# A vision transformer block on one core: V computed once by token, sent through DRAM into a layout by image, and masked by GpSimd

## The reference

```python
h = patchify(x) @ W_proj.T + b_proj + pos_emb          # 16 x 36 x 256, cls_tok ahead: S = 37
qkv = layernorm(h) @ W_qkv + b_qkv
q, k, v = split into 16 heads of 16
att = softmax(causal(q k^T / 4)); out = att @ v         # within one image
h = h + out @ W_out + b_out
z = layernorm(h)                                        # each token goes to one of 8 experts
h = h + score * (gelu(z @ w1[e] + b1[e]) @ w2[e] + b2[e])
```

## Time and profile before

| | us |
|---|---|
| runs shown | 195.72, 196.68, 396.79 |
| their median | 196.68 |
| profiled execution, first to last instruction (span) | 193.6 |
| TensorE busy | 149.7 (77%) |
| VectorE busy | 81.2 (42%) |
| ScalarE busy | 50.5 (26%) |
| GpSimd busy | 30.9 (16%) |
| mean DMA rate over the span | 139 GB/s |

### The profile page before, as it was taken

How to read it: one execution, slowest core, us unless ns; L and a number is a source line. 1 busy time by engine, 2 the same in 40 slices (tenths; PEclk the granted TensorE clock), 3 DMA queues, 4 the chain that set the end, 5 groups by cost and what they waited for, 6 DMA issues and landing times.

```text
span 193.6 us, 2570 instructions
## 1 busy us (share of the span) xinstructions
PE 149.7 (77%) x937; PEld 121.8 (63%) x937; DVE 81.2 (42%) x243; ACT 50.5 (26%) x137; POOL 30.9 (16%) x41
## 2 busy tenths in 40 slices
PE   0006999898499999999984540188999999999980
PEld 0005688676357676686673430178999999999960
DVE  0011002876966678767885348714212022022030
ACT  0002001409513442424432010007421421431400
POOL 1010001496000001001011100430030430420222
PEclk9999999999999999999999655559999999999999
DMA  6999999300000000100681110240059999940000
GB/s 190 372 361 372 377 377 381 107 3 0 0 0 0 2 3 2 54 3 0 186 301 58 56 54 0 71 145 4 0 181 344 352 318 335 349 156 0 18 19 24
DMA packets 15696, 26.99 MB, mean 139 GB/s; under 512 B 2253, under 2 KB 11012, under 8 KB 15552
## 3 DMA queue, kind: packets, MB, share of 16 engines
q1 hardware_dynamic: 12624, 21.89, 32.5%
q0 software_dynamic: 1024, 2.71, 4.2%
q10 hardware_dynamic: 2032, 2.19, 3.4%
HBM read 24.86 MB, written 2.36 MB: 141 GB/s over the span
## 4 chain that ended last, share of the span: by engine, by line
PE 73%; DVE 10%; DMA 8%; issue 2%; ACTq 2%; ACT 2%; POOL 1%; POOLq 0%; DVEq 0%
PE ps L652 16%; PE ps L664 14%; PE ps L515 8%; PE ps L462 8%; DMA bqk<-b_qk 6%; PE ps L532 5%; PE ps L558 4%; PE ps L544 3%; PE ps L606 3%; PE ps L495 3%; PE ps L460 2%; DVE wide L740 2%; DMA early<-hz_scratch,growu 2%; PE ps L535 2%; PE ps L640 1%
## 5 line engine op out<-in xcount | busy, mean ns | idle before, releaser
L652 PEld LDWEIGHTS ps<-early,w1s 128*128 128x128 f32 x256 | 31.7, 203 | 2.2 <-issue 1.9
L652 PE MATMUL ps<-early,w1s 128*128 128x128 f32 x256 | 32.0, 287 | 1.3 <-DVE early L879 1.3
L664 PE MATMUL ps<-w2s,early 128*128 128x256 f32 x128 | 28.8, 379 | 0.0
L431 ACT ACTIVATE early<-ps,b1s 128x128 f32<-128x128 f32 x64 | 18.2, 371 | 31.8 <-PE ps L652 31.8
L664 PEld LDWEIGHTS ps<-w2s,early 128*128 128x128 f32 x128 | 23.8, 190 | 2.9
L952 POOL DMA_INDIRECT out<-early,srowu x8 | 8.1, 1008 | 49.0 <-DVE early L892 49.0
L462 PE MATMUL ps<-early 128*128 128x256 f32 x60 | 14.9, 414 | 0.0
L887 DVE TENSOR_TENSOR ysum<-ps,b2s 128x256 f32<-128x256 f32 x8 | 3.4, 425 | 26.7 <-PE ps L664 26.7
L462 PEld LDWEIGHTS ps<-early 128*128 128x128 f32 x60 | 12.5, 211 | 2.6 <-issue 0.7
L395 ACT ACTIVATE probs<-shifted 101x296 f32<-101x296 f32 x16 | 7.2, 451 | 24.8 <-DVE shifted L762 24.8
L879 DVE COPY early<-ps 128x256 f32<-128x256 f32 x8 | 3.4, 425 | 22.7 <-PE ps L640 22.7
(11 more groups left out here) (125 smaller groups left out, 196.3 us busy)
## 6 DMA issues: line engine op xcount, KB each, us to landing
w1s<-w SPq DMA_DIRECT2D x8, 1024.0 KB, 5.3
w2s<-w SPq DMA_DIRECT2D x8, 1024.0 KB, 9.4
early<-embed_in SPq DMA_DIRECT2D x6, 448.0 KB, 8.9
hz_scratch<-hz SPq DMA_DIRECT2D x5, 256.0 KB, 2.3
b2s<-b ACTq DMA_DIRECT2D x1, 1024.0 KB, 19.9
wqkv<-w_qkv SPq DMA_DIRECT2D x1, 768.0 KB, 13.0
cf<-const_f ACTq DMA_DIRECT2D x1, 642.0 KB, 11.2
wout<-w_out SPq DMA_DIRECT2D x1, 256.0 KB, 13.4
```

Source lines behind the costliest of these rows:

```text
L431: nc.scalar.activation(gt[:, t % 2, f, :], ps[:, 2 * (t % 2) + f // 4, (f % 4) * P:(f % 4 + 1) * P], ACT.Gelu, bias=b1t[:, f:f + 1]).then_ ...
L652: m = nc.tensor.matmul(ps[:, 2 * (t % 2) + f // 4, (f % 4) * P:(f % 4 + 1) * P], w1s[:, r, k, f * P:(f + 1) * P], xt[:, t % 2, k, :], star ...
L664: m = nc.tensor.matmul(ps[:, 4 + t % 2, 0:D], gt[:, t % 2, f, :], w2s[:, r, f, :], start=(f == 0), stop=(f == FT - 1))
```

## The change

V is computed once for each token. `value_rows(j)` on TensorE multiplies a tile of `xnt` by the V columns, ahead of and among the Q and K matmuls. ScalarE copies the result to `vrow`, the first half of `hz`. SP stores it to a DRAM scratch `v_scratch` in two parts (tiles 0 to 2, tiles 3 and 4), waits for each store, and loads it back by image, `[37 rows, 8 images, 256]`, three times a half, to partitions 0, 37 and 74 of `v3`, in the slot where `thrice` was. GpSimd multiplies by `vmask` and writes `vbd`, for all eight pairs, ahead of its adds to `h`. `thrice`, `values` on TensorE and `values` on VectorE go. The load of expert 2 moves behind the V loads, that of expert 3 waits for GpSimd's `v_ready`. scores(0) waits for both parts of Q. The third group of an attend takes its own 34 columns, not 51 for each image.

```diff
+        v_d = nc.dram_tensor("v_scratch", [TP, D], F32, kind="Internal").ap()
-        thrice = [w[:, RING - 1, :, :].rearrange("p a b -> p (a b)")[:, 0:B * GS] for w in (w1s, w2s)]
+        vrow = hz[:, :, 0:D]
+        v3 = [w[0:GS, RING - 1, :, :].rearrange("p a b -> p (a b)").rearrange("p (b d) -> p b d", d=D)
+              for w in (w1s, w2s)]
+        HALF_T = -(-(T // 2) // P)
+        VALUES = ((0, 2, 6), (2, 3, 3), (3, 5, 3))
...
@@ SP
-            for t in range(RING - 1):
-                load_expert(t)
+            load_expert(0)
+            load_expert(1)
+            for g, (j0, j1) in enumerate(((0, HALF_T), (HALF_T, NT))):
+                sp.wait_ge(q["vrow_ready"], j1)
+                sp.dma_start(v_d[j0 * P:j1 * P, :].rearrange("(j p) d -> p j d", p=P), vrow[:, j0:j1, :])\
+                  .then_inc(q["vrow_stored"], 16)
+                sp.wait_ge(q["vrow_stored"], 16 * (g + 1))
+                b0, b1_ = g * B // 2, (g + 1) * B // 2
+                for r in range(GH):
+                    sp.dma_start(v3[g][r * S:(r + 1) * S, :, :],
+                                 v_d[b0 * S:b1_ * S, :].rearrange("(b s) d -> s b d", s=S)).then_inc(loaded_v[g], 16)
+            load_expert(2)
...
-                    sp.wait_ge(q["v_ps"], PAIRS)
+                    sp.wait_ge(q["v_ready"], PAIRS)
...
@@ TensorE
+            def value_rows(j):
+                pe.wait_ge(q["xnt_ready"], j + 1)
+                if j == HALF_T:
+                    pe.wait_ge(q["vrow_ready"], HALF_T)
+                v0, _, bank = next(v for v in VALUES if v[0] <= j < v[1])
+                for k in range(KD):
+                    m = nc.tensor.matmul(ps[:, bank, (j - v0) * D:(j - v0 + 1) * D], xnt[:, k, j * P:(j + 1) * P], wqkv[:, k, 2 * D:3 * D],
+                                         start=(k == 0), stop=(k == KD - 1))
+                m.then_inc(q["vrow_ps"], 1)
...
+                    if a == 0 and n == 1:
+                        pe.wait_ge(q["vrow_ready"], 2)
+                    if a == 1 and n == 2:
+                        pe.wait_ge(q["vrow_ready"], NT)
...
-                    pe.wait_ge(q["q_ready"], u + 1)
+                    pe.wait_ge(q["q_ready"], KD)
...
+                    w = min(GH, HH - g * GH) * VW
...
@@ GpSimd
+            pool.wait_ge(q["v_zeroed"], 2)
+            for pair in range(PAIRS):
+                pool.wait_ge(loaded_v[pair // (PAIRS // 2)], 16 * GH)
+                pool.tensor_tensor(
+                    vbd[:, 2 * pair * VI:2 * (pair + 1) * VI].rearrange("p (h w) -> p h w", w=VW)[:, :, 0:DH],
+                    v3[pair // (PAIRS // 2)][:, 2 * (pair % (PAIRS // 2)):2 * (pair % (PAIRS // 2)) + 2, :].rearrange("p a (h w) -> p (a h) w", w=DH),
+                    C("vmask")[0:GS, :].unsqueeze(2).to_broadcast([GS, 2 * HEADS, DH]), ALU.mult).then_inc(q["v_ready"], 1)
 
             pool.wait_ge(q["loaded_bout"], 16)
             for j in range(NT):
```

More of the change, by code:

```diff
@@ L274, in vit_tower @@
             loaded_bv loaded_bout loaded_b1 loaded_b2 loaded_wg loaded_wred
-            embedded h_saved veps_ready rstd_ready xn_ready xnt_ps xnt_ready thrice_ready
+            embedded h_saved veps_ready rstd_ready xn_ready xnt_ps xnt_ready vrow_ps vrow_ready vrow_stored
             wg_sq wg_norm wgn_ready wgnt_ps wgnt_ready g_ps g_ready bqs_ready
-            qk_ps k_ready q_ready kbd_dve kbd_act v_zeroed v_ps v_ready pads_ready
+            qk_ps k_ready q_ready kbd_dve kbd_act v_zeroed v_ready pads_ready
             scores_ps shifted_ready probs_ready probst_ps probst_ready o_ps o_ready ot_ps ot_ready
@@ L285, in vit_tower @@
         loaded_emb = [sem(f"loaded_emb{k}") for k in range(KE)]
+        loaded_v = [sem(f"loaded_v{g}") for g in range(2)]
         loaded_w = [sem(f"loaded_w{r}") for r in range(RING)]
@@ L362, in _ @@
                 nc.scalar.activation(h[:, j, :], ps[:, j, 0:D], ACT.Copy).then_inc(q["h_saved"], 1)
[L363 to L372, removed]
+            for j0, j1 in ((0, HALF_T), (HALF_T, NT)):
+                for j in range(j0, j1):
+                    act.wait_ge(q["xnt_ps"], j + 1)
+                    nc.scalar.activation(xnt[:, :, j * P:(j + 1) * P],
+                                         ps[:, 5 + 2 * (j % 2), 0:KD * P].rearrange("p (k n) -> p k n", k=KD),
+                                         ACT.Copy).then_inc(q["xnt_ready"], 1)
+                for v0, v1, bank in VALUES:
+                    if j0 < v1 <= j1:
+                        act.wait_ge(q["vrow_ps"], v1)
+                        nc.scalar.activation(vrow[:, v0:v1, :],
+                                             ps[:, bank, 0:(v1 - v0) * D].rearrange("p (j d) -> p j d", d=D),
+                                             ACT.Copy).then_inc(q["vrow_ready"], v1 - v0)
             act.wait_ge(q["bqs_ready"], 1)
@@ L482, in turn_normalised @@
                 m.then_inc(q["xnt_ps"], 1)
+            def value_rows(j):
[7 more added lines that the diff above has]
+                m.then_inc(q["vrow_ps"], 1)
             HALF = T // 2
-            for j in range(-(-HALF // P)):
+            for j in range(HALF_T):
                 turn_normalised(j)
@@ L490, in _ @@
             pe.wait_ge(q["g_ready"], 1)
-            pe.wait_ge(q["xnt_ready"], -(-HALF // P))
+            for j in range(HALF_T):
+                value_rows(j)
             for a in range(2):
                 for n, (col, bank) in enumerate(((D, 0), (D + P, 6), (0, 2), (P, 4))):
+                    if a == 0 and n == 1:
+                        pe.wait_ge(q["vrow_ready"], 2)
+                    if a == 1 and n == 2:
+                        pe.wait_ge(q["vrow_ready"], NT)
                     for k in range(KD):
@@ L499, in _ @@
                 if a == 0:
-                    for j in range(-(-HALF // P), NT):
+                    for j in range(HALF_T, NT):
                         turn_normalised(j)
[L502 to L517, removed]
+                    for j in range(HALF_T, NT):
+                        value_rows(j)
             def scores(u):
@@ L555, in attend @@
                     col = 2 * pair * VI + (c * HH + g * GH) * VW
-                    rhs = early[0:GS, col:col + 2 * VI].rearrange("p (a n) -> p a n", a=2)[:, :, 0:GH * VW]
+                    w = min(GH, HH - g * GH) * VW
+                    rhs = early[0:GS, col:col + 2 * VI].rearrange("p (a n) -> p a n", a=2)[:, :, 0:w]
                     dst = ps[0:ROWS, BO + u % 2, 0:2 * CH * GH * VW].rearrange("p (a n) -> p a n", a=2)
-                    m = nc.tensor.matmul(dst[:, :, g * GH * VW:(g + 1) * GH * VW],
+                    m = nc.tensor.matmul(dst[:, :, g * GH * VW:g * GH * VW + w],
                                          probst[:, u % 2, g * ROWS:(g + 1) * ROWS], rhs, start=True, stop=True)
@@ L568, in _ @@
             pe.wait_ge(q["pads_ready"], 1)
-            values(0)
             for i in range(STEPS):
@@ L572, in _ @@
                     scores(i)
-                    if i % 2 == 0 and i // 2 + 1 < PAIRS:
-                        values(i // 2 + 1)
                 if 0 <= i - 1 < UNITS:
@@ L583, in _ @@
                     pe.wait_ge(q["zt_ready"], j + 1)
-                    if j == EARLY:
-                        pe.wait_ge(q["v_ready"], PAIRS)
                     for k in range(KD):
@@ L741, in _ @@
                                     C("kmask")[:, hd:hd + 1], None, ALU.mult).then_inc(q["kbd_dve"], 1)
[L743 to L753, removed]
             for i in range(STEPS):
```

## The result

The changed kernel takes 259.51 us (259.06 to 261.79, 4 runs) against 196.22 us before: ratio 1.324, 95% interval 1.317 to 1.331. The profiled execution took 259.93 us with a span of 258.1. All ratios here are of the undisturbed executions of either kernel; the one of before that took 396.79 us counts in its median of 196.22 and in no ratio.

A forecast was written before the change was run, and what follows sets the result against it. TensorE was taken to bound the attention loop, VectorE just behind. With the slow V loads, transposed(8) at 140.5 plus 110.5 gives 251.0, plus 2.3 for clock 253.3, plus 3.1 outside the span 256.4 us; range 240 to 270.

The forecast's parts named there:

- One engine for 37 rows: V loads from DRAM: all six share one DMA engine, 46.5 ns a row, 41.3 us a half plus 1.4 fixed.
- two engines for 38 rows: Reading of the early sel transfer: its 38 rows went out on two DMA engines, not on 16.
- The store of half 1 behind half 0: SP's queue: the store of V's half 1 lands only about 1.7 us after half 0's loads, at 88.7.
- Masks: GpSimd's mask of each pair: two 128x256 adds of 0.70 us, 1.4 us for 512 columns.
- The second stall is GpSimd's queue ahead of attend(8): Masks queued ahead of the bout adds hold VectorE's hz of step 7 to 137.9, transposed(8) to 140.5.
- The clock at the restart: After 30 us of standing, TensorE resumes the loop at half clock, booked at 2.3 us.
- the time outside the span: Median less span, 3.1 us in the kernel before, added again to the forecast span of 253.3 us.
- The bounds written for the range: Whole kernel: row pace, clock, store round trip, mask length and lone-engine pace, together 244 to 270 us.
- The first rival: V loads spread over most DMA engines and the change does what it says: 188.1 us, chance 0.07.
- the engines' own gain of 8.6 us: Engines alone: 10.3 us from the loop and 2.0 at its start, less 3.7 for added TensorE matmuls.
- The second rival, the lock: Loads spread, but GpSimd's masks and VectorE's kbd copies shut each other out, some 8 us: 196.1 us, chance 0.04.
- steps near 2.0 us there: Sign of being right: attention loop steps take near 2.0 us between the stalls.

The follow-up runs named there:

- E1: The changed kernel with each load of 37 rows cut into one of 32 rows and one of 5: 200.51 us, ratio 1.019.
- e2: The changed kernel with each load of 37 rows cut into one of 34 rows and one of 3: 220.91 us, ratio 1.124.
- e3: The changed kernel with GpSimd's five adds of bout to h put ahead of its eight masks: 256.39 us, ratio 1.302.
- e9: The changed kernel with GpSimd's adds ahead of all masks and the second normalisation's first power ahead of pair 4's mask: 247.80 us, ratio 1.267.
- e8: The changed kernel with 68 extra matmuls, results unused, ahead of the transposes of unit 8: 255.60 us, ratio 1.300.
- e11: The changed kernel with loads of 32 and 5 rows, masks after the kbd copies, four extra matmuls ahead of each of scores(0) and scores(1): 187.33 us, ratio 0.957.
- e6: The changed kernel with loads of 32 and 5 rows, and GpSimd's masks waiting for VectorE's thirteen kbd copies: 198.58 us, ratio 1.010.
- e5: The changed kernel with loads of 32 and 5 rows, five extra matmuls ahead of scores(0), six ahead of scores(1): 188.87, 200.29, 201.57 and 202.53 us.

## Why the prediction was right, point by point

- **One engine for 37 rows**: right, and the heart of it. Half 0 took 42.6 us where 41.3 + 1.4 = 42.7 was forecast, that is 46.4 ns a row. E1 and e2 show that the outer size decides. This is what the Trainium skill ("DMA: Bandwidth & Descriptors", "Why a DMA increments its semaphore by 16 and not by 1") states, and its rule was worth more here than the two rows of `sel` alone. Those came from a stretch of 0.03 us with a DMA share of 0.52, which by itself would be eight engines, so the reading "two engines for 38 rows" was thin; e2's 34 rows at 45 GB/s are what shows two. That the three loads of a half share an engine is shown by 22 GB/s with all of them in flight.
- **The store of half 1 behind half 0**: right, landed at 88.4 against 88.7. Half 1 took 45.3 us, 2.6 more than half 0. The load of expert 2 ran beside its end (140 GB/s from 120 to 130 us), which would explain it but was not tried.
- **Masks**: 1.06 us each, not 1.4; the strided and broadcast operands cost GpSimd nothing that shows. 1.5 us less in the sum.
- **The second stall is GpSimd's queue ahead of attend(8)**: right, `hz` at 138.7 against 137.9, and e3 with e9 show it. What I had not seen is that the power stands in the same queue, one step behind the adds, and that attend(8) would have stalled the loop for 19.7 us even so (e9): the order was worth about 11 us, the slow second half the rest.
- **The clock at the restart**: right in kind, too small. Booked 2.3 us, measured about 5.0 (e8). I had taken the price from the experts, whose dense matmuls win the clock back within one of them; the loop's did not until an output projection.
- **The sum, and luck in it**: the span was 4.8 us over the forecast's 253.3. 0.9 of them lie ahead of transposed(8) (141.4 against 140.5), 2.7 are the clock term, and 1.2 are the rest of the kernel at full clock, 111.7 us in e8 against the 110.5 booked; no run separates these 1.2. The median was off by only 3.1 us, partly because of an error the other way: the time outside the span, booked as 3.1 us from a median and the span of another execution, is 1.8 in the profiled execution (259.93 - 258.1) and 1.7 to 2.0 in all others; that takes 1.3 off, and the profiled execution's 0.4 us above the median are the rest. The bounds written for the range do not add up to it either: -3.6, -2.3 and -3 give 247.5 at the low end, not 244. The measured time lies inside both.
- **The first rival's 188.1 us**, the engines' own gain of 8.6 us: e11 has 187.3, with loads spread, masks late and the clock held. The spread loads alone (e1) left the kernel about 2% behind the one before, so that rival would have failed as written.
- **The second rival, the lock**: real, 2.4 us and not 8, since half of the masks came after the copies and a mask held a copy up by 0.6 us. The Trainium skill ("SBUF — State Buffer", "Who interferes with whom") has the loser blocked for the whole instruction; that is how the memset of 3.74 us acted, while beside these masks of 1.32 us the loss was about half a mask each on average. The longest copy took 1.33 us instead of 0.52, so it lost 0.8 of a mask's 1.32; whether a copy waited out what was left of a mask or ran slower beside it, no row here tells.

What the prediction did not have at all is that the loop without value matmuls would run at half clock between the stalls; its own sign of being right, steps near 2.0 us there, failed. In the changed kernel it was hidden in part: steps 3 to 7 ran at half clock (0.50 from 90 to 108), but ended before the wait for `hb_ready`, which covered them.

## What to carry to other kernels

Look at the outer dimension of a transfer before its bytes: 909 KB in loads of 37 rows took 42.6 us on one DMA engine, and the same bytes cut into 32 and 5 rows were no longer felt. When work moves into an engine's queue, read what stands behind it there, to the end: here adds, then a power, each held the whole loop. And matmuls that are taken out of a full TensorE may have been holding its clock (not tried by itself here: the runs show that filling the waits ahead of the loop held it), so price what is left at both levels, and look for the stretch ahead of it in which the engine waits.

## What the runs showed of the hardware that was not expected

- The loop's own matmuls, with TensorE busy without a gap, did not raise the clock from 1.2 to 2.4 GHz for 23 us (e1, 60 to 83 us). In the changed kernel at 107.7 and 151.6, in e1 at 83.1 and in e9 at 139.3 an output projection ran, and the clock was full 2 to 3 us after each began. Why then, no run here separates.
- Across waits of 1.66 and 2.08 us ahead of the loop the clock was lost in e6 and in the changed kernel, while the kernel before kept it through one of 2.89 us that value matmuls followed (L515 at 51.23). In e5, with such waits filled for the most part, one execution of four took 188.9 us and three 200 to 203.
- An issue on SP can last long behind slow transfers: 13.4 us for the store of half 1 in the changed kernel, 0.39 in e1.
